# Layer stage of a decoder kernel: both halves of heads scored and weighted in one phase each, token shift by transfers, new orders

## The reference, cut to what matters

```python
def shift_tokens(t):                        # second half of the channels comes from the token before
    a, s = jnp.split(t, 2, -1)
    s = jnp.pad(s, ((0, 0), (1, 0), (0, 0)))[:, :-1]
    return jnp.concatenate([a, s], -1)
for i in range(6):
    x = attn_layer(shift_tokens(x), Wqkv[i], q_scale[i], k_scale[i], Wo[i]) + x   # 16 heads of 64
    x = ffn_layer(shift_tokens(x), ln_g[i], ln_b[i], W1[i], b1[i], W2[i], b2[i]) + x
```

## Time and profile before

| | us |
|---|---|
| median of 3 runs | 4595.98 |
| lowest, highest | 4591.91, 4602.75 |
| the profiled execution, device time | 4600.57 |
| its span (first to last instruction) | 4598.8 |

### The profile page before, as it was taken

One profiled execution on the slowest core, in us unless ns is written; L12 is line 12 of the kernel. 1 busy time (PEld: TensorE's weight loads), 2 busy tenths in 40 slices (PEclk: granted clock), 3 DMA queues, 4 the chain that ended last, 5 costly groups with the idle time before them and its releaser, 6 DMA issues.

```text
span 4598.8 us, 149905 instructions
## 1 busy us (share of the span) xinstructions
PE 4426.6 (96%) x61616; PEld 3422.3 (74%) x61616; DVE 3567.7 (78%) x11101; ACT 3495.8 (76%) x9695; POOL 2653.1 (58%) x2208
## 2 busy tenths in 40 slices
PE   7999989999999999999999999999999779999999
PEld 5777667777777777777777777777777568888888
DVE  4666599888888888888888888888888556666675
ACT  3555488888888888888888888888888546766776
POOL 3444377777676676766667666777667323333332
PEclk9898799999999999999999999999999869999999
DMA  3000000000000000000000000000000100000000
GB/s 97 4 4 4 3 2 2 2 2 2 25 2 2 2 25 2 2 2 2 25 2 2 2 25 2 2 2 6 4 6 7 45 1 4 4 4 4 4 4 6
DMA packets 40195, 40.16 MB, mean 9 GB/s; under 512 B 4164, under 2 KB 37976, under 8 KB 38744
## 3 DMA queue, kind: packets, MB, share of 16 engines
q1 hardware_dynamic: 39512, 30.59, 2.2%
HBM read 28.48 MB, written 2.10 MB: 7 GB/s over the span
## 4 chain that ended last, share of the span: by engine, by line
PE 89%; DVE 6%; ACT 3%; issue 1%; POOL 0%; SPq 0%; DMA 0%; ACTq 0%; DVEq 0%; POOLq 0%
PE ps L532 73%; PE ps L536 16%; ACT BIG L885 2%; DVE BIG L1086 2%; DVE sm L1097 1%; DVE BIG L1094 1%; ACT L885 1%; DVE BIG L1091 1%; POOL BIG L1523 0%; ACT BIG L877 0%; DVE sm L1094 0%; POOL sm L1526 0%; DVE BIG L1164 0%; DVE sm L1090 0%; DVE sm L1193 0%
## 5 line engine op out<-in xcount | busy, mean ns | idle before, releaser
L877 ACT ACTIVATE BIG<-ps 128x512 f32<-128x512 f32 (+6 forms) x3216 | 1480.7, 505 | 608.5 <-PE ps L536 441.5
L532 PE MATMUL ps<-WB,BIG 128*128 128x128 f32 (+1 forms) x8576 | 1896.6, 363 | 7.8 <-DVE BIG L1086 5.5
L1523 POOL TENSOR_TENSOR BIG<-BIG,sm 128x1024 f32<-128x1024 f32 (+1 forms) x864 | 1223.2, 1425 | 745.5 <-DVE sm L1094 503.3
L532 PEld LDWEIGHTS ps<-WB,BIG 128*128 128x128 f32 x8576 | 1152.8, 192 | 410.2 <-issue 378.2
L532 PEld LDWEIGHTS ps<-BIG 64*64 64x64 f32 (+2 forms) x37888 | 944.0, 131 | 294.2 <-issue 193.7
L1523 POOL TENSOR_TENSOR BIG<-BIG 128x512 f32<-128x512 f32 x768 | 974.2, 1276 | 323.5 <-DVE BIG L1086 322.7
L532 PE MATMUL ps<-BIG 64*64 64x64 f32 (+4 forms) x37888 | 1071.2, 225 | 24.1 <-DVE BIG L1164 8.4
L1097 DVE TENSOR_REDUCE sm<-BIG 128x8 f32<-128x512 f32 (+3 forms) x1472 | 872.7, 617 | 140.0 <-ACT BIG L885 133.1
L536 PE MATMUL ps<-t_ident,BIG 128*128 128x128 f32 x6016 | 873.7, 282 | 94.1 <-DVE BIG L1094 42.2
L536 PEld LDWEIGHTS ps<-t_ident,BIG 128*128 128x128 f32 x6016 | 707.7, 144 | 253.9 <-issue 108.2
L885 ACT ACTIVATE BIG<-ps,sm 128x64 f32<-128x64 f32 (+1 forms) x3104 | 678.5, 330 | 103.4 <-DVE sm L1097 100.8
(11 more groups left out here) (121 smaller groups left out, 3054.3 us busy)
## 6 DMA issues: line engine op xcount, KB each, us to landing
WB<-in_Wqkv SPq DMA_DIRECT2D x6, 1536.0 KB, 7.5
y_sb<-in_ctx SPq DMA_DIRECT2D x16, 256.0 KB, 2.9
WB<-in_Wo SPq DMA_DIRECT2D x6, 512.0 KB, 8.9
x_sb<-in_x SPq DMA_DIRECT2D x8, 256.0 KB, 5.4
WB<-in_F_W SPq DMA_DIRECT2D x1, 2048.0 KB, 8.6
WB<-in_F_W SPq DMA_DIRECT2D x8, 256.0 KB, 6.2
out<-x_sb SPq DMA_DIRECT2D x8, 256.0 KB, 2.3
WB<-in_W SPq DMA_DIRECT2D x6, 341.0 KB
```

The lines of the kernel that those rows point to most:

```text
L532: return te.matmul(o, l, r, start=start, stop=stop, skip_group_check=not check)
L877: return se.activation(o, i, ACT.Copy)
L1523: return pe_.tensor_tensor(o, a, b, op)
```

## The change

1. `s` of both halves becomes one TensorE phase of 32 matmuls, and `y`, `w` become one phase of 16 matmuls each. Half 1 swaps the column halves in its scores (its rows of the score bank are exchanged, and `w` and `y` of half 1 take the other sequence first), so that four matmuls in a row lie in four different quarters. The phase waits for what both halves need. `y` takes two of the six handed-round banks, and holds them until ScalarE's `o0` and `o1`.
2. The token shift leaves TensorE and ScalarE: two DMAs per C2 unit, issued by SyncE, write the shifted half into a new buffer `XS`; ScalarE copies only the plain half. VectorE's `tr` writes a second buffer instead of working in place. SyncE's loads of weights and context are put between the shifts.
3. All four orders are new; other lags, hence other distances between producers and users of a buffer.

```diff
 C_ORDER = {
-    "pe": "2a25 1v14 1k02 1x1 1k12 1v02 2o6 1o6 1b03 1a03 1q01 1p15 1p04 2g23 1b13 2g03 2sh1 2a14 2g13 2a03 "
-          "1a13 1q11 1s03 1y15 1y04 1s13 1w15 1w04 2tr2",
+    "pe": "2tr3 1v13 2a16 1k12 1p15 2o6 1o6 1b03 1a03 1q01 2g03 2g13 2g23 1b13 1a13 2a03 1v03 2a23 1p04 1q11 "
+          "1y5 1w5 1s3 1x0 1k01",
+    "act": "1b04 1q02 1a04 1b14 2g04 2g14 2g24 1f04 1f14 1a14 1q12 1v04 2sh2 1p05 1o06 1o16 1x1 1k02 1s04 1k12 "
+           "2tr3 1s14 1v13 1p15",
+    "dve": "1first0 1n42 1n52 1n62 1n72 1i14 1n82 2a23 1r01 1q11 1s03 1r11 2a15 1s13 1k01 1l01 1u03 1o5 1k11 "
+           "2sh1 2ag1 1i03 1l11 2o5 2ep1 1u13 1n01 1q00 1n11 1n21 2tr1 1n31 2a02 1second1",
+    "pool": "1first1 1n13 1q12 1k02 1q02 1p04 1k12 2sh2 1p14 1n02",
...
+                if u.kind == "C1" and ph == "y":
+                    u.after[ph] = []
+                    for h in "01":
+                        u.bank["y" + h] = turn % 6
+                        u.after[ph] += full[turn % 6] or []
+                        full[turn % 6] = [(u, "act", "o" + h)]
+                        turn += 1
...
+            def shift(l, g):
+                for i in range(4):
+                    w.wait_ge(*uC1[(l, 4 * g + i)].on("dve", "o"))
+                if g or l:
+                    w.wait_ge(*uC2[(l, g - 1) if g else (l - 1, 7)].on("dve", "tr"))
+                for r in (0, 64):
+                    eng.dma_start(XS[r + 1:r + 64, :, 64:128], y_sb[r:r + 63, 4 * g:4 * g + 4, 64:128]).then_inc(sems["shift"], 16)
...
+            def half(hf, par):
+                return slice(64 * (par ^ hf), 64 * (par ^ hf) + 64)
...
+                elif ph == "s":
+                    for m in ("a0", "b0", "f0", "a1", "b1", "f1"):
+                        w.wait_ge(*u.on("act", m))
+                    for i in range(8):
+                        for hf in range(2):
+                            b, K = c_bufs(u, hf), bank[u.bank[f"s{hf}"]]
                             for par in range(2):
+                                c, r = slice(64 * i, 64 * i + 64), slice(64 * par, 64 * par + 64)
+                                o = mm(K[half(hf, par), c], b.qT[r, c], b.kT[r, c], start=False, stop=i == 7, check=False)
...
+                elif ph in "yw":
+                    for m in ("p0", "v0", "p1", "v1"):
+                        w.wait_ge(*u.on("act", m))
...
                     for i in range(8):
                         hp, par = i // 2, i % 2
+                        for hf in range(2):
+                            b, K, bb = c_bufs(u, hf), bank[u.bank[f"y{hf}"]], (hf + (ph == "w")) % 2
+                            q, r = slice(64 * bb, 64 * bb + 64), half(hf, par)
+                            o = mm(K[64 * par:64 * par + 64, 256 * bb + 64 * hp:256 * bb + 64 * hp + 64],
+                                   b.VV[q, 64 * i:64 * i + 64], b.PT[q, 128 * hp + r.start:128 * hp + r.stop])
...
                 if ph == "sh":
-                    w.wait_ge(*u.on("pe", "sh"))
...
-                    copy(x4[:, :, 64:128], K[:, 0:256].rearrange("p (t d) -> p t d", d=64))
-                    o = copy(x4[:, :, 0:64], y_sb[:, 4 * g:4 * g + 4, 0:64])
+                    o = copy(XS[:, :, 0:64], y_sb[:, 4 * g:4 * g + 4, 0:64])
```

More of the change, by code:

```diff
@@ L307, in build @@
         names += [f"x{i}" for i in range(8)] + [f"c{i}" for i in range(8)] + ["k_" + s for s in SETS]
-        names += ["wat0", "wat1", "wq", "wf", "wm", "out", "const", "y0", "rot0", "rot1", "rope", "ones", "prime", "half"]
+        names += ["wat0", "wat1", "wq", "wf", "wm", "out", "const", "y0", "rot0", "rot1", "rope", "ones", "prime", "half", "shift"]
         sems = {n: ctx.enter_context(nc.semaphore("s_" + n)) for n in names}
@@ L410, in build @@
             for u, ph in c_phases("pe", n):
-                if u.kind == "C1" and ph[0] == "s":
-                    u.bank[ph], u.after[ph] = 6 + int(ph[1]), ()
+                if u.kind == "C1" and ph in "sw":
+                    u.bank.update({"s0": 6, "s1": 7} if ph == "s" else {})
+                    u.after[ph] = ()
                     continue
-                if u.kind == "C1" and ph[0] == "w":
-                    u.bank[ph], u.after[ph] = u.bank["y" + ph[1]], ()
+                if u.kind == "C1" and ph == "y":
[5 more added lines that the diff above has]
+                        turn += 1
                     continue
@@ L489, in ffn_weights, with context @@
                     eng.dma_start(WB[0:n, O2 + 128 * i:O2 + 128 * i + 128], din["W2"][l, r0:r0 + n, :]).then_inc(sems["wf"], 16)
+            def shift(l, g):
[5 more added lines that the diff above has]
+                    eng.dma_start(XS[r + 1:r + 64, :, 64:128], y_sb[r:r + 63, 4 * g:4 * g + 4, 64:128]).then_inc(sems["shift"], 16)
+            def context(i):
+                w.wait_ge(*uC2[(depth - 1, i)].on("dve", "x"))
+                eng.dma_start(c_sb[:, 4 * i:4 * i + 4, :], cv[:, 4 * i:4 * i + 4, :]).then_inc(sems[f"c{i}"], 16)
             if "C" in stages:
+                attn_weights(0)
+                ffn_weights(0)
+                attn_weights(1)
                 for l in range(depth):
[L493 to L503, removed]
+                    for g in range(8):
+                        shift(l, g)
+                        if g == 0 and l:
+                            w.wait_ge(*uC2[(l - 1, 7)].on("pe", "o"))
+                            ffn_weights(l)
+                            if l + 1 < depth:
+                                for s in qkv_free(l - 1):
+                                    w.wait_ge(*s)
+                                attn_weights(l + 1)
+                        if g >= 2 and l == depth - 1 and "E" in stages:
+                            context(g - 2)
+                for i in (6, 7) if "E" in stages else ():
+                    context(i)
                 for s in qkv_free(depth - 1) + [uC2[(depth - 1, 7)].on("pe", "o")]:
@@ L671, in pe_bank @@
                     w.wait_ge(*v.on(e, m))
-                return bank[u.bank[ph]]
+                return bank[u.bank[ph]] if ph in u.bank else None
+            def half(hf, par):
+                return slice(64 * (par ^ hf), 64 * (par ^ hf) + 64)
             def pe_c1(u, ph):
@@ L735, in pe_c2 @@
                 K, b = pe_bank(u, ph), c2_bufs()
[L736 to L741, removed]
+                if ph == "tr":
                     w.wait_ge(*u.on("dve", "tr"))
                     for i in range(4):
-                        o = tr(K[:, 128 * i:128 * i + 128], b.xs[:, 128 * i:128 * i + 128])
+                        o = tr(K[:, 128 * i:128 * i + 128], b.xn[:, 128 * i:128 * i + 128])
                     o.then_inc(u.name("pe", ph, sems), 1)
@@ L939, in act_c1 @@
                 b = c_bufs(u, int(h) if h in "01" else 0)
-                K = bank[u.bank[{"o": "w", "f": "s"}.get(ph[0], ph[0]) + ph[1:]]]
+                K = bank[u.bank[{"o": "y", "f": "s"}.get(ph[0], ph[0]) + ph[1:]]]
                 two, three, four = before(u, 2), before(u, 3), before(u, 4)
@@ L1301, in dve_c2 @@
                 b, st, mv, sm = c2_bufs(), st_[4], mv_[4], sm_[4]
-                xs = [b.xs[:, 128 * i:128 * i + 128] for i in range(4)]
                 if ph == "sh":
                     w.wait_ge(*u.on("act", "sh"))
+                    w.wait_ge("shift", 32 * (8 * l + g + 1))
+                    w.wait_ge("ones", 1)
                     for i in range(4):
-                        o = ve.bn_stats(st[:, i, :], xs[i])
+                        o = ve.bn_stats(st[:, i, :], XS[:, i, :])
                 elif ph == "ag":
@@ L1584, in ones_row @@
                     w.wait_ge(*s)
+                for r in (0, 64):
+                    pe_.memset(XS[r:r + 1, :, 64:128], 0.0)
                 pe_.memset(c2_bufs().hT[64:96, 1024:1536], 1.0).then_inc(sems["ones"], 1)
```

48 lines of the change are left out of this document (17 added, 31 removed), and 5 rows, old and new, of the table C_ORDER.

## The result

Median 4445.45 us (4434.89 to 4465.72, four runs) against 4594.66 beside it: ratio 0.9673 [0.9651, 0.9695], 149 us less. Forecast were 4239, with a range of 4200 to 4390: the sign was right, the time lies above the range. The profiled execution took 4434.89 (span 4433.1), 165.7 less than the one of before.

What follows compares the result with a forecast made beforehand. TensorE was taken to bound the layer stage: 63.5 us per group less 7.2 (matmuls) and 0.43 (shift), plus 0.1 lateness, gives 56.0. Over 48 groups 360 us less, 3 more at the end: median 4239, range 4200 to 4390.

Steps and rivals of the forecast that it cites:

- own work: TensorE's time per layer-stage group if it never waited, forecast to fall from 63.5 to 55.9 us.
- What bounds it: Layer stage: TensorE, busy 508.02 of 508.02 us, sets the period; ScalarE and VectorE were not expected to become the bound.
- Four quarters run together: Scores and weighted values: four 64 x 64 matmuls run at a time instead of two, 7.2 us less per group.
- the price of a round: Scores and weighted values: a round of four matmuls takes 58 ns, nearly the 57.2 of a round of two.
- (b): Scores and weighted values: four quarters do not run together at 64 wide; only the shift gains, 4578 us; chance 0.06.
- (c): Score banks cannot take two row halves at once, so `s` stays narrow; half the 7.2 won, 4404 us; chance 0.03.
- The size of that term: Scores and weighted values per group: 256 rounds, 14.6 us, become 128 rounds, 7.4 us; 7.2 us less.
- The shift: Token shift, once per group: its matmul leaves TensorE, 0.43 us less, the DMAs covered except at the stage's end.
- I allow 0.1 us of lateness a group: Layer stage: addition to TensorE's 55.9 us for waits on other engines, giving a 56.0 us period; bounds 0 and 7.6.
- Rival (a): Layer stage: ScalarE or VectorE becomes late each group and TensorE waits, 2 to 4 us lost, 4380 us; chance 0.19.
- Rival (d): Layer stage: joined `s` closes a loop, ScalarE idles for the maxima in each C1 unit, 4692 us; chance 0.03.
- Filling and emptying the stage: Layer stage's ends: 2 to 3 us more at the end for uncovered DMAs; filling may move 5 us either way.

Runs made afterwards that it cites:

- run 3: Changed kernel with one tiny exponential on ScalarE behind gelu g2, bringing the group's second table load forward: 4404.61 us, ratio 0.9594.
- run 6: Changed kernel with seven eighths of ScalarE's mask left out, so results are not the reference's: 4426.63 us, ratio 0.9624.
- run 7: Changed kernel with seven eighths of VectorE's sum of squares left out, so results are not the reference's: 4422.41 us, ratio 0.9615.
- run 12: run 3 with seven eighths of GpSimd's adds of the rotated parts left out, so results are not the reference's: 4352.7 us, ratio 0.9473.
- run 5: Kernel before the change, old orders, with only the token shift moved to two DMAs per C2 unit: 4566.32 us, ratio 0.9927.
- run 2: Changed kernel with TensorE's `s` put between `y` and `w`: 4482.36 us, ratio 0.9763.
- run 9: run 3 with the next unit's two `k0` matmuls put between `y` and `w` in TensorE's order: 4420.43 us, ratio 0.964.
- run 14: run 3 with VectorE's `n0` reading one operand and the next unit's `k0` between `y` and `w`: 4428.18 us, ratio 0.965.
- run 8: run 3 with VectorE's reciprocal `i1` moved ahead of three Newton steps: 4454.36 us, ratio 0.9688.
- run 13: run 3 with VectorE's step `n0` written as a tensor_scalar with one operand in place of two: 4392.72 us, ratio 0.9573.

## Why the prediction was wrong

The period was forecast as 63.5 - 7.2 - 0.43 = 55.9 of own work and 0.1 of lateness. Point by point:

- **What bounds it: right for the kernel before, wrong for the changed one.** It is no longer TensorE's work alone: relief of ScalarE (runs 3 and 6), of VectorE (run 7) and of GpSimd (run 12) each shortened it.
- **Four quarters run together: right, and the price of a round too.** (2.34 - 0.15 - 0.32)/32 = 58.4 ns against the forecast 58. Rivals (b) and (c) are out: `s` takes 1.09 us for 16 rounds, (1.09 - 0.15)/16 = 58.8 ns, the same as the rest. The Trainium skill's 25 ns from start to start (TensorE: Matmul & The Clock Gate, section "Wait — 56ns, not 53.3ns?") would make 3.2 us of 128 instructions; 2.34 were measured.
- **The size of that term: off by 1.3.** Measured are 4 x (3.81 - 2.34) = 5.9 us a group, forecast 7.2. What I left out is in the code of before already: `w` waits for the last matmul of `y`. In the earlier trace rows `s` or another half's phase stood between them; `1y5 1w5` puts them side by side, and the wait shows, 0.32 us, four times a group: 1.28 us, 61 in 48 groups. The step "256 x 57.2 = 14.6 becomes 128 x 58 = 7.4 us" counted rounds and not the drain between them (the 0.306 us from the last start of `y` to the first of `w`).
- **The shift: right.** 0.43 forecast, 0.43 measured (run 5), with no wait for the transfers but at the stage's end.
- **The step that failed most: "I allow 0.1 us of lateness a group".** Own work is then 63.5 - 5.9 - 0.4 = 57.2; the period is 60.07 in the 24 groups shown, so 2.9 us are lateness there, and 3.1 over the stage. 2.38 of the 2.9 show as TensorE idle (91.24 us in 2300), 1.1 at `b1` alone. The rest would be waits too short to show as idle; for that speaks that TensorE is busy 57.8 us a group here and 57.4 in run 12, with the same instructions. I had weighed each engine's total against the period (92 and 96%) and the mean time of a bank (4.2 us against a rotation of 2.7). Neither sees an order: the bank of `b1` was late because of what stood ahead of one copy. Runs 3, 6 and 7 show it: the load moved brings 41 us, twice and four times as much load taken away brings 19 and 23.
- **Rival (a) was the right mechanism, at 2 to 4 us lost a group and a chance of 0.19.** Lost were 60.07 - 56.0 = 4.1, with the drain, and 4.3 over the stage, so that even its slowest time, 4428, is passed by 17. It looked at ScalarE and VectorE only; GpSimd, busy 44.2 of 63.5, was left out, and run 12 puts its adds at some 1.1 us a group. The range ended at 4390, inside this rival's own 4332 to 4428. Its "Against", that they never hold TensorE up in the earlier trace rows, was drawn from a kernel with one slow engine and says nothing of a balanced one.
- **Rival (d)** fell: ScalarE's waits for the maxima are 4.4 us in all, the joined `s` does not close a loop.

In sum, with the stage's mean period of 60.33: 48 x 1.3 = 62 us are the matmul term, 48 x (60.33 - 57.2 - 0.1) = 145 the lateness, together 208. Filling and emptying the stage came out 10 better than forecast and the other stages 7 shorter, which leaves the 191 by which the profiled execution lies above its forecast of 4243.6. The median lies 206 above, because it is 10.6 over the profiled execution, where I had put it 4.6 under.

Of the lateness, the table load's place is 41 us (run 3) and GpSimd's load another 52 (run 12). In run 12 the mean period is 58.27 (37 groups from 1032.52 to 3188.54), of which TensorE is busy 98.5%, 57.4: close to the own work as summed above, 57.2. Some 1 us a group of lateness is left there, without a run of its own. Runs 2, 9 and 14 do not contradict this. Putting another phase between `y` and `w` looked like own work saved, but the traces show 0.12 us saved of 0.32 in run 2 and nothing in run 9, while the phases behind came later. Why that costs as much as 16 to 37 us is open; removing the wait itself was not tried, since `y` and `w` would then write one bank from two halves of the rows unordered.

## What to carry to other kernels

When the one full engine is relieved until the others stand at 90% and more, forecast the new period from the queues, not from busy totals: for each buffer or bank handed round, list what stands ahead of the instruction that frees it, table loads included. Where an order is rewritten, look for phases that must wait for each other's last result and now stand side by side, and count that wait (0.32 us each time here). Before counting on its removal, read in a trace whether the stretch with another phase in between is really shorter: here it was hardly so, and the phases behind it came later. A table load, or any work with a free place, goes where nothing that is awaited queues behind it: 41 us here for one tiny activation.

## What the runs showed of the hardware

**VectorE's small SBUF steps stand still beside GpSimd, for whole instructions.** A 128x32 step from and to SBUF takes 0.19 us; started while a GpSimd block of 128x512 is running it takes up to 1.02 (run 8; 1.15 in run 3) and ends 0.05 us behind the block. In the changed kernel that holds for all 73 long ones; the 77 that started up to 0.02 us ahead of a block kept their 0.19. Which of the two comes first decides. In 1000 to 3300 us there are 42 such steps over 0.3 us before, 73 in the changed kernel, 189 in run 8, and none with the adds cut (run 12):

```profile
L1121 DVE SCALAR_TENSOR_TENSOR sm<-sm 128x32 f32<-128x32 f32 x766 | 278.8, 364 | 20.6
```
```profile
L1121 DVE SCALAR_TENSOR_TENSOR sm<-sm 128x32 f32<-128x32 f32 x790 | 149.5, 189 | 21.2
```

The first row is run 8, the second run 12. It holds for a float32 step with one SBUF operand as well (run 13); a reduction from SBUF (0.67 us) and a multiplication with a PSUM operand (0.41) take in the changed kernel the same median time beside a GpSimd instruction (605 and 967 instances) and without one. The Trainium skill, SBUF — State Buffer, section Terms, says of the shared port pair of the two engines that it is an exclusive lock, held for the full instruction; the trace agrees, 1.02 us against 0.19. Whether the loss of run 8 is this lock or the order itself is not settled: with the adds cut its long steps fell from 189 to 117 only, and the distance of 50 us to its partner stayed (54).

**Four 64 x 64 quarters at once** take 58 ns a round, as long as two in the kernel before (57.2). In `s` two row halves write into one bank meanwhile, each into its own column half, at the same 58.8 ns.
